# Building one-hot tables in half the steps, with GpSimd taking half of the scaling, in a mixture-of-experts and linear-attention kernel

## Chip, cores and metric

The kernel runs on one core of one Trainium2 chip. The metric is the device time of one launch in microseconds (us); lower is better. Engines are named as in the profile: PE is TensorE, DVE is VectorE, ACT is ScalarE, POOL is GpSimd, SP is SyncE, which only issues DMAs here.

## The reference

Input x has 16 sequences of 512 tokens of 128 features (8192 tokens). After a layer norm, two branches read the same tokens, and their product is added to x.

```python
xn = _layernorm(x, axis=-1)
s = attn(xn)      # token shift, r/k/v projections, 16 heads of 8, chunked decaying state, output projection
g = silu(ffn(xn)) # gates = softmax(xn @ gate_W.T), top 2 of 8 experts
# expert:  (silu(t @ w1_e) * (t @ w3_e)) @ w2_e, width 512, weighed by the gates, 2 per token
# shared:  the same form with w1_s, w3_s, w2_s, applied to all tokens, divided by 8
# ffn = 0.5 * shared + 0.5 * routed
return x + s * g
```

## The kernel before

**Stages.** Normalisation and transposes come first, with the routing logits. Then a feed-forward stage of 62 units, and then 16 attention units. Each matrix product in the feed-forward stage is made of three half-precision products, from a high half and a low half of each operand.

**Units and steps.** A shared unit takes 512 tokens in their own order and is four steps, one for each 128 hidden columns. There are 16. A routed unit takes tokens sorted by expert: 25 wide units (512 rows, four steps) and 21 narrow ones (256 rows, two steps). That makes 206 steps. The list `order` starts with `FIRST = 16 - MIXED` shared units; with `MIXED = 4` these are 12 units, or `FIRST_STEPS = 48` steps (0 to 47). The other four shared units stand among the routed ones. Sorted rows are counted in blocks of 256, 71 in all.

**One step i.** PE makes the two up projections (`pe_up`, 6 matmuls of 512 columns). ACT takes the silu (L781). DVE multiplies it by the second projection (L1218; one input in SBUF, one in PSUM). ACT rounds the product to its high half (L785). The low half is a subtraction of two SBUF tensors, on DVE (`dve_split`, L1222) or on POOL (`pool_first_low`, L624), as `low_on_pool(i)` says: before the change POOL has steps 0 to 11 and then each even step up to 38. PE makes the down projection three steps later (`pe_down`, `LAG = 3`). `pe_up(i)` waits for L1218 of step i-2, and L1218 of step i waits for the low half of step i-2, since `gu` has two buffers.

**Sorting.** To find which token stands in which sorted row, the kernel builds one-hot tables in 16 sets m: `dve_block_set(m)` (L1141, 128x1136, both inputs in SBUF) and `dve_lane_set(m)` (L1151, 128x1024, the same). The block table is scaled by token numbers in two halves of 128x568 (`act_tokens`, L823, two instructions a set). PE multiplies lanes by blocks, 128 products (`pe_hot`, L1498). A set's block table is built in the step that `slot_of` gives, from `HOT_FIRST = 13` over `HOT_SLOTS = 24` steps, its lane table and scaling one step later, and its products at `HOT_LAG = 3`. Behind the last product `dve_source` (L1161 to L1174) makes the gather indices in step 39 and `dve_dest` (L1178 to L1185) the scatter indices in step 40.

**Gather and scatter.** POOL issues two indirect DMAs of 128 rows for each block: gathers into the ring `srows` of `NXB = 3` blocks (`pool_sorted`, L634) and, seven blocks later in its queue, scatters of results (`pool_scatter`, L644). PE transposes a gathered block (`pe_sorted`, L1509, "flip") in the steps of the unit before. The first flip is in step 46 before the change.

**Other work in the steps.** Expert weights come in through a stage of two experts. ACT makes the high halves (`act_split_w`, L766), DVE the low halves (`dve_split_w`, L1013, both inputs in SBUF). `SPLIT_AT` gives the steps: 16 parts over steps 1 to 36 and 8 parts in steps 40 to 47. SP loads expert k only when all parts of expert k-2 are split. The first routed unit waits for all weights. `act_route` (L770, L771, with table loads) stands in step 26 and `dve_gates` (L1201 to L1207) in step 29. From step 75 each fourth step carries a part of the attention projections (`pe_part`, L1596), 32 in all.

Of the kernel before, what the change touches and what calls it, by code (L numbers as in the profile page):

```python
# [69 lines left out]
def build(nc, nb, x, decay, per_head, maa, wT, bias, bias_rows, gateT, w1e, w3e, w2e, w1s, w3s, w2s, const, out):  # L70
# [18 lines left out]
    with ctx:  # L89
# [64 lines left out]

        NXB = 3
        srows = sb("srows", [P, NXB, TPU, P])
# [27 lines left out]
        NBLK = ROUTED * TPU  # L184
        SETS, LANES, LANE_SETS, BLOCK_SETS = 16, 2 * NT // 16, 4, 3
        FOUR = LANES // 2
# [31 lines left out]
        wtmp = early([P, HEADS, Q])  # L218
        same = late([P, HEADS, Q])
        w32r = early([P, P])  # L220
# [70 lines left out]

        MIXED = 4
        FIRST = SHARED - MIXED
# [69 lines left out]
        NHOTS = 2 * NT  # L363
        HOT_FIRST, HOT_SLOTS, HOT_LAG = 13, 24, 3

# [22 lines left out]
        def low_on_pool(i):  # L388
            return i < LOWS_FIRST or (i < HOT_FIRST + HOT_SLOTS + HOT_LAG and i % 2 == 0)

        def lows(i, on_pool):
            return sum(low_on_pool(j) == on_pool for j in range(i + 1))

        LOWS_FIRST = 12
        FIRST_SPLIT = 14
# [9 lines left out]

        LAST_SPLITS = 8
        EARLY_SPLITS = 3 * EXPERTS - LAST_SPLITS
        SPLIT_AT = [1 + j * 38 // EARLY_SPLITS for j in range(EARLY_SPLITS)]
        SPLIT_AT += [FIRST_STEPS - LAST_SPLITS + j for j in range(LAST_SPLITS)]

# [193 lines left out]
        def pool_program(e):  # L604
# [17 lines left out]
            def pool_first_low(i):  # L622
                G.wait_ge(sem["gu_hi"], i + 1)
                G.tensor_tensor(gul[:, i % 4, :], gu[:, i % 2, :], guh[:, i % 4, :], ALU.subtract).then_inc(sem["gu_lo_first"], 1)  # L624

            def pool_sorted(q):
                if q == 0:
                    G.wait_ge(sem["normed_out"], 16 * nb)
                    G.wait_ge(sem["source"], 1)
                if q >= NXB:  # L630
                    G.wait_ge(sem["s_flipped"], q - NXB + 1)
                for t in range(TPU):
                    at = block_at[q] * TPU + t
                    G.indirect_dma_start(srows[:, q % NXB, t, :], None, rows_in,  # L634
                                         bass.IndirectOffsetOnAxis(source[:, at:at + 1], 0)
                                         ).then_inc(sem[f"s_in{q % NXB}"], 16)

# [65 lines left out]
            for b in range(nb):  # L703
                pool_norm(b)
            for i in range(FIRST_STEPS):
                if low_on_pool(i):
                    pool_first_low(i)
# [25 lines left out]
        def act_program(e):  # L733
# [85 lines left out]
            def act_tokens(m):  # L819
                A.wait_ge(sem["hot_block"], m + 1)  # L820
                for k in range(2):
                    half = hot_block[:, m % BLOCK_SETS, k * FOUR:(k + 1) * FOUR, :]
                    A.mul(half, half, C("token")[:, 16 * k + m:16 * k + m + 1]).then_inc(sem["hot_token"], 1)  # L823

# [624 lines left out]
        def pe_program(e):  # L1449
# [44 lines left out]
            def pe_hot(n):  # L1494
                m, k, g = hot_of(n)
                T.wait_ge(sem["hot_set"], m + 1)
                T.wait_ge(sem["hot_token"], 2 * m + k + 1)
                T.matmul(psum[6 + g // 2][:, g % 2 * NBLK:(g % 2 + 1) * NBLK], hot_lane[:, m % LANE_SETS, n % LANES, :],  # L1498
# [230 lines left out]
            for i in range(NS + LAG):  # L1729
                if i < NS:  # L1730
                    pe_up(i)
                    if i == ROUTE_AT:
                        pe_route()
                    for n in hots(i - HOT_FIRST - HOT_LAG):
                        pe_hot(n)
                    for q in flips_at(i):
                        pe_sorted(q)
                if i >= LAG:
                    load = steps[i][0] + 1 if i < NS and last_step_of(i) and routed(steps[i][0] + 1) else None
                    pe_down(i - LAG, load)  # L1740
                if i < NS and part_at(i) is not None:
                    pe_part(part_at(i))
# [47 lines left out]
```

## Time and profile before

| what | value |
|---|---|
| median of 3 runs | 722.61 us |
| runs | 722.04, 722.61 and 2308.06 us |
| span of the profiled execution | 719.3 us |
| PE, DVE, ACT, POOL busy | 91%, 77%, 69%, 67% of the span |
| mean granted TensorE clock | 0.988 |

The span runs from the first to the last instruction of the profiled execution. No separate launch time is listed for that execution; the median lies 3.3 us above its span, and that is taken as what lies around it. The run of 2308.06 us stands alone.

### The profile page before, as it was taken

What the parts mean: (1) busy time and instruction counts of PE and PEld (TensorE: products, weight loads), DVE (VectorE), ACT (ScalarE), POOL (GpSimd) and SP (SyncE); (2) the same over time, 40 slices, a digit from 0 to 9 for tenths busy, and PEclk for the clock granted to TensorE, in tenths of its full rate; (3) what the DMA queues carried; (4) which work ended last, traced back from release to release, by engine and by line L of the source; (5) the groups of instructions that cost most, each with busy time, mean ns of one, the idle gap of its engine ahead of it and who ended that gap; (6) DMA issues with size and microseconds to landing.
All of it is one profiled execution on the core that took longest, in us unless ns stands there. A gap on an engine that the chain in (4) does not pass through costs nothing.

```text
span 719.3 us, 22370 instructions
## 1 busy us (share of the span) xinstructions
PE 654.1 (91%) x8536; PEld 452.1 (63%) x8536; DVE 555.4 (77%) x1058; ACT 494.9 (69%) x1008; POOL 478.9 (67%) x519
## 2 busy tenths in 40 slices
PE   2787897978999999999999999999997899999993
PEld 1544565646665665566666666878886676777772
DVE  5989986877667886667766676667664899999996
ACT  4864798857665656666666666666665788888872
POOL 4844321244777777777777777767778487888873
PEclk9999999999999999999999999999999999999997
DMA  9931111111111323433323334333362767777762
GB/s 243 299 95 45 45 61 46 45 51 36 48 49 49 108 91 108 137 108 108 110 92 109 106 106 139 110 101 108 97 103 93 237 179 230 216 229 222 233 176 59
DMA packets 88616, 86.75 MB, mean 121 GB/s; under 512 B 11394, under 2 KB 65284, under 8 KB 88516
## 3 DMA queue, kind: packets, MB, share of 16 engines
q1 hardware_dynamic: 79428, 66.70, 29.8%
q0 software_dynamic: 9088, 18.63, 9.6%
q8 instruction: 73, 1.20, 0.7%
q14 instruction: 27, 0.22, 0.1%
HBM read 50.82 MB, written 34.47 MB: 119 GB/s over the span
## 4 chain that ended last, share of the span: by engine, by line
PE 53%; DVE 13%; ACT 12%; POOL 11%; issue 7%; DMA 3%; SPq 0%; POOLq 0%; DVEq 0%; ACTq 0%
PE banks L1556 7%; PE banks L1558 7%; PE banks L1557 7%; PE banks L1596 5%; DVE hidden L1218 4%; POOL expert_rows L644 4%; PE banks L1576 4%; PE banks L1577 4%; PE banks L1575 4%; POOL srows L634 3%; ACT hidden L785 3%; PE banks L1621 3%; PE banks L1693 3%; PE banks L1672 3%; ACT rows L823 2%
## 5 line engine op out<-in xcount | busy, mean ns | idle before, releaser
L785 ACT CAST hidden<-hidden 128x512 f16<-128x512 f32 x206 | 127.1, 617 | 135.5 <-DVE hidden L1218 135.4
L634 POOL DMA_INDIRECT srows<-normed_rows,source x142 | 149.7, 1054 | 60.4 <-issue 40.2
L1222 DVE TENSOR_TENSOR hidden<-hidden 128x512 f16<-128x512 f32 x180 | 124.4, 691 | 83.9 <-ACT hidden L785 83.0
L1218 DVE TENSOR_TENSOR hidden<-hidden,banks 128x512 f32<-128x512 f32 x206 | 140.8, 684 | 44.0 <-ACT hidden L781 38.2
L1575 PE MATMUL banks<-wwords,hidden 128*128 (+1 forms) x824 | 148.8, 219 | 1.5 <-DVE hidden L1222 1.1
L1576 PE MATMUL banks<-wwords,hidden 128*128 (+1 forms) x824 | 148.6, 219 | 0.0
L1577 PE MATMUL banks<-wwords,hidden 128*128 (+1 forms) x824 | 148.6, 219 | 0.0
L781 ACT ACTIVATE hidden<-banks 128x512 f32<-128x512 f32 x206 | 122.7, 596 | 28.1 <-PE banks L1558 27.8
L1556 PE MATMUL banks<-sx,wwords 128*128 128x512 f16 (+1 forms) x368 | 121.5, 330 | 3.2 <-DVE wwords L1013 2.7
L1558 PE MATMUL banks<-sx,wwords 128*128 128x512 f16 (+1 forms) x368 | 121.6, 330 | 0.0
L1557 PE MATMUL banks<-sx,wwords 128*128 128x512 f16 (+1 forms) x368 | 121.5, 330 | 0.0
L644 POOL DMA_INDIRECT expert_rows<-ybuf,dest x72 | 77.2, 1072 | 22.8 <-issue 19.8
L1575 PEld LDWEIGHTS banks<-wwords,hidden 128*128 128x128 f16 x824 | 80.6, 98 | 12.4 <-issue 2.0
L644 POOL DMA_INDIRECT expert_rows<-rows,dest x70 | 72.8, 1040 | 23.1 <-issue 20.1
L1576 PEld LDWEIGHTS banks<-wwords,hidden 128*128 128x128 f16 x824 | 80.6, 98 | 11.3
L624 POOL TENSOR_TENSOR hidden<-hidden 128x512 f16<-128x512 f32 x26 | 33.6, 1294 | 76.8 <-ACT hidden L785 76.8
L1303 DVE TENSOR_TENSOR wwords<-banks,wmat 128x1024 f32<-128x1024 f32 x64 | 75.3, 1217 | 10.9 <-PE banks L1672 10.5
L1577 PEld LDWEIGHTS banks<-wwords,hidden 128*128 128x128 f16 x824 | 80.6, 98 | 0.0
L1556 PE MATMUL banks<-xh,wwords 128*128 128x512 f16 x128 | 49.2, 385 | 19.1 <-DVE hidden L1218 18.7
L1321 DVE SCALAR_TENSOR_TENSOR hidden<-banks,cst,hidden 128x256 f32<-128x256 f32 x128 | 61.5, 481 | 3.8 <-ACT hidden L849 0.7
L1558 PEld LDWEIGHTS banks<-sx,wwords 128*128 x368 | 36.0, 98 | 25.6
L1557 PE MATMUL banks<-xl,wwords 128*128 128x512 f16 x128 | 49.0, 383 | 0.0
(218 smaller groups left out, 1429.7 us busy)
## 6 DMA issues: line engine op xcount, KB each, us to landing
rows<-x SPq DMA_DIRECT2D x32, 256.0 KB, 4.9
rows<-expert_rows SPq DMA_DIRECT2D x32, 256.0 KB, 3.6
normed_rows<-rows SPq DMA_DIRECT2D x16, 256.0 KB, 3.9
r_rows<-rows SPq DMA_DIRECT2D x16, 256.0 KB, 2.1
rd_rows<-rows SPq DMA_DIRECT2D x16, 256.0 KB, 2.2
stage<-r_rows SPq DMA_DIRECT2D x16, 256.0 KB, 4.0
k_rows<-rows SPq DMA_DIRECT2D x16, 256.0 KB, 2.2
kd_rows<-rows SPq DMA_DIRECT2D x16, 256.0 KB, 2.2
```

Of the source, the lines that this page charges most:

```text
L634: G.indirect_dma_start(srows[:, q % NXB, t, :], None, rows_in, bass.IndirectOffsetOnAxis(source[:, at:at + 1], 0)).then_inc(sem[f"s_in{q % ...
L644: G.indirect_dma_start(rows_out, bass.IndirectOffsetOnAxis(dest[:, at:at + 1], 0), ring_of(q)[:, t, :], None).then_inc(sem[f"y_stored{q % ...
L781: A.activation(sg[:, i % 2, :], psum[2 * (i % 2)][:, :], ACT.Silu, scale=1.0 / SW).then_inc(sem["silu"], 1)
L785: A.copy(guh[:, i % 4, :], gu[:, i % 2, :]).then_inc(sem["gu_hi"], 1)
L1218: V.tensor_tensor(gu[:, i % 2, :], sg[:, i % 2, :], psum[2 * (i % 2) + 1][:, :], ALU.mult).then_inc(sem["gated"], 1)
L1222: V.tensor_tensor(gul[:, i % 4, :], gu[:, i % 2, :], guh[:, i % 4, :], ALU.subtract).then_inc(sem["gu_lo"], 1)
L1556: T.matmul(o, a, mh, start=True, stop=False)
L1557: T.matmul(o, a, ml, start=False, stop=False)
L1558: k = T.matmul(o, b, mh, start=False, stop=True)
L1575: T.matmul(o, guh[:, i % 4, s], a, start=(j == 0 and n == 0), stop=False)
L1576: T.matmul(o, guh[:, i % 4, s], b, start=False, stop=False)
L1577: k = T.matmul(o, gul[:, i % 4, s], a, start=False, stop=last)
```

## The change

The tables are built over 12 steps in place of 24, one step nearer to their products. POOL scales the second half of each block table, and ACT only the first. POOL makes all low halves of steps 0 to 26, and DVE makes all from step 27 on. `MIXED` becomes 8, so 8 shared units (32 steps) precede the first routed one, and the other 8 stand among the routed units. The gather ring has six blocks. The weight parts stand in other steps: 14 in steps 1 to 25 and 10 in steps 27 to 31, two a step. The block table has four buffers, and the products stand behind the step's down projection.

```diff
-        NXB = 3
+        NXB = 6
-        SETS, LANES, LANE_SETS, BLOCK_SETS = 16, 2 * NT // 16, 4, 3
+        SETS, LANES, LANE_SETS, BLOCK_SETS = 16, 2 * NT // 16, 4, 4
-        same = late([P, HEADS, Q])
+        same = rows[:, 0:HEADS * Q // P, :].rearrange("p a (c i) -> p (a c) i", i=Q)
-        MIXED = 4
+        MIXED = 8
-        HOT_FIRST, HOT_SLOTS, HOT_LAG = 13, 24, 3
+        HOT_FIRST, HOT_SLOTS, HOT_LAG = 13, 12, 2
         def low_on_pool(i):
-            return i < LOWS_FIRST or (i < HOT_FIRST + HOT_SLOTS + HOT_LAG and i % 2 == 0)
+            return i < HOT_FIRST + HOT_SLOTS + HOT_LAG
-        LOWS_FIRST = 12
-        LAST_SPLITS = 8
+        LAST_SPLITS = 10
-        SPLIT_AT = [1 + j * 38 // EARLY_SPLITS for j in range(EARLY_SPLITS)]
-        SPLIT_AT += [FIRST_STEPS - LAST_SPLITS + j for j in range(LAST_SPLITS)]
+        SPLIT_AT = [1 + j * 26 // EARLY_SPLITS for j in range(EARLY_SPLITS)]
+        SPLIT_AT += [FIRST_STEPS - LAST_SPLITS // 2 + j // 2 for j in range(LAST_SPLITS)]
+            def pool_tokens(m):
+                G.wait_ge(sem["hot_block"], m + 1)
+                half = hot_block[:, m % BLOCK_SETS, FOUR:2 * FOUR, :]
+                G.tensor_scalar(half, half, C("token")[:, 16 + m:17 + m], None, ALU.mult).then_inc(sem["hot_token1"], 1)
             for i in range(FIRST_STEPS):
+                for m in block_sets(i - 1):
+                    pool_tokens(m)
                 if low_on_pool(i):
                     pool_first_low(i)
             def act_tokens(m):
                 A.wait_ge(sem["hot_block"], m + 1)
-                for k in range(2):
-                    half = hot_block[:, m % BLOCK_SETS, k * FOUR:(k + 1) * FOUR, :]
-                    A.mul(half, half, C("token")[:, 16 * k + m:16 * k + m + 1]).then_inc(sem["hot_token"], 1)
+                half = hot_block[:, m % BLOCK_SETS, 0:FOUR, :]
+                A.mul(half, half, C("token")[:, m:m + 1]).then_inc(sem["hot_token0"], 1)
             def pe_hot(n):
-                T.wait_ge(sem["hot_token"], 2 * m + k + 1)
+                T.wait_ge(sem[f"hot_token{k}"], m + 1)
                     if i == ROUTE_AT:
                         pe_route()
-                    for n in hots(i - HOT_FIRST - HOT_LAG):
-                        pe_hot(n)
                     for q in flips_at(i):
                         pe_sorted(q)
                 if i >= LAG:
                     load = steps[i][0] + 1 if i < NS and last_step_of(i) and routed(steps[i][0] + 1) else None
                     pe_down(i - LAG, load)
+                for n in hots(i - HOT_FIRST - HOT_LAG):
+                    pe_hot(n)
```

## Rows read from the trace of the kernel before

**Rows 1.** Busy time in four stretches: start:end, length, then each engine.
```profile
42.80:76.80 34.00, 26.58 (x215) 15.02 (x214) 32.70 (x63) 18.60 (x35) 16.12 (x12) 1.00 0.10 30
76.80:110.90 34.10, 30.65 (x294) 19.99 (x293) 30.36 (x50) 28.25 (x51) 8.68 (x7) 1.00 0.16 55
110.90:172.50 61.60, 50.69 (x463) 32.78 (x462) 48.63 (x89) 47.96 (x85) 18.35 (x15) 0.97 0.16 48
172.50:545.00 372.50, 368.09 (x3416) 256.74 (x3415) 260.66 (x435) 240.15 (x465) 282.33 (x269) 1.00 0.32 98
```

**Rows 2.** Timeline of ACT, silus of steps 27, 48, 161 and 162: start, duration.
```profile
117.22 0.60 ACT L781 ACTIVATE hidden<-banks 128x512 f32<-128x512 f32 x1
...
172.51 0.60 ACT L781 ACTIVATE hidden<-banks 128x512 f32<-128x512 f32 x1 [1.61 <-PE banks L1558]
...
440.21 0.60 ACT L781 ACTIVATE hidden<-banks 128x512 f32<-128x512 f32 x1
...
442.18 0.60 ACT L781 ACTIVATE hidden<-banks 128x512 f32<-128x512 f32 x1
```

**Rows 3.** Timeline of DVE in step 20, away from POOL: start, duration.
```profile
97.62 0.68 DVE L1013 SCALAR_TENSOR_TENSOR wwords<-stage,wwords 128x512 f16<-128x512 f32 x1
98.22 0.68 DVE L1151 TENSOR_TENSOR rows<-sx 128x1024 f16<-128x1024 f16 x1
98.82 0.74 DVE L1141 TENSOR_TENSOR rows<-sx 128x1136 f16<-128x1136 f16 x1
```

**Rows 4.** Timeline of all engines where a POOL subtraction meets DVE's lane table.
```profile
133.86 1.43 POOL L624 TENSOR_TENSOR hidden<-hidden 128x512 f16<-128x512 f32 x1 [3.77 <-ACT hidden L785]
134.31 0.69 DVE L1218 TENSOR_TENSOR hidden<-hidden,banks 128x512 f32<-128x512 f32 x1
...
134.38 0.48 PE L1498 MATMUL banks<-rows 128*128 128x142 f16 x5
134.91 0.93 DVE L1151 TENSOR_TENSOR rows<-sx 128x1024 f16<-128x1024 f16 x1
```

**Rows 5.** Timeline where DVE's L1013 meets a POOL subtraction near its start.
```profile
52.06 1.25 POOL L624 TENSOR_TENSOR hidden<-hidden 128x512 f16<-128x512 f32 x1 [0.31 <-ACT hidden L785]
...
52.22 1.64 DVE L1013 SCALAR_TENSOR_TENSOR wwords<-stage,wwords 128x512 f16<-128x512 f32 x1
```

**Rows 6.** POOL's groups by shape: count, busy us, mean ns, idle before.
```profile
L634 POOL DMA_INDIRECT srows<-normed_rows,source x142 | 149.7, 1054 | 60.4 <-issue 40.2 <-PE banks L1509 14.5 <-DVE source L1174 5.7
...
L619 POOL TENSOR_SCALAR rows<-rows,ffn 128x128 f32<-128x128 f32 x48 | 22.3, 476 | 8.1 <-DVE ffn L1000 7.2
...
L698 POOL TENSOR_TENSOR rows<-rows 128x512 f32<-128x512 f32 x15 | 19.2, 1279 | 2.2 <-DVE rows L1330 2.2
...
L650 POOL MEMSET stage<- 128x1024 f32 x1 | 1.0, 971 | 0.0
```

**Rows 7.** Timeline of DVE in step 39, `dve_source` from first to last.
```profile
150.21 0.72 DVE L1161 TENSOR_SCALAR ybuf<-banks 128x142 f32<-128x142 f32 x3
...
153.71 0.68 DVE L1218 TENSOR_TENSOR hidden<-hidden,banks 128x512 f32<-128x512 f32 x1
```

**Rows 8.** DMA issues by tile: median us to landing.
```profile
stage<-w2e SPq DMA_DIRECT2D x8, 256.0 KB, 3.8
```

**Rows 9.** The chain that ended last: an attention part and a flip.
```profile
368.73 1.32 PE banks L1596 x6
...
371.34 0.22 PE banks L1509 x2
```

**Rows 10.** Waits at line L1509: PE idle in total, times.
```profile
  DMA srows<-normed_rows,source: 8.8, 7
```

**Rows 11.** Timeline of ACT: the last unit's result.
```profile
548.88 0.37 ACT L807 COPY rows<-banks 128x256 f32<-128x256 f32 x1 [1.54 <-PE banks L1577]
```

**Rows 12.** Timeline of POOL and SP: the last scatter, the second key load.
```profile
554.04 0.97 POOL L644 DMA_INDIRECT expert_rows<-rows,dest  x1 [0.31 <-issue]
...
557.98 0.43 SPq L519 DMA_DIRECT2D wwords<-kd_rows  x1
```

## The prediction

> **What bounds the kernel now.** I first cut the span at the silus of certain steps and asked for busy time in each stretch [rows 1]. The reader is to see that PE is the bound only from step 48 on: from 172.5 to 545 us it is busy 368.1 of 372.5 us. In steps 0 to 12 (42.8 to 76.8) DVE is busy 32.7 of 34.0, and in steps 13 to 25 it is busy 30.4 of 34.1, with ACT at 28.3. So the first 48 steps hang on DVE and ACT. They take 129.7 us, while PE alone would need 48 x 1.97 = 94.6; 1.97 is a step with neither flip nor attention part, the distance of steps 161 and 162 [rows 2]. Then I read single instructions where POOL and DVE overlap, since the change puts more on POOL beside DVE.
>
> **What a POOL operation does to DVE.** Left alone, DVE starts its operations 0.60 us apart, 0.08 less than they last: L1013 at 97.62, L1151 at 98.22, L1141 at 98.82 [rows 3]; L1141, 0.06 longer, then costs 0.66. In one place POOL's subtraction runs from 133.86 to 135.29. L1218, with one input in PSUM, runs beside it in its usual 0.69. L1151, both of whose inputs are in SBUF, takes 0.93 and ends at 135.84, 0.55 behind POOL's end [rows 4]. Where L1013 meets the subtraction near its start it takes 1.64 in place of 0.68 [rows 3, 5]. So one low half on POOL costs DVE up to 1.64 - 0.68 = 0.96 us, unless DVE is in L1218 or idle. The subtraction itself lasts between 1.25 and 1.43 here [rows 4, 5]; undisturbed I put it at 1.16 (estimate: DVE's second one ends 0.55 behind it, so POOL too will have waited for a table operation at its start).
>
> The Trainium skill, "SBUF — State Buffer", section "Who interferes with whom", says that a VectorE instruction with two SBUF inputs contends with a GpSimd instruction that reads SBUF, and that the later one blocks fully. By that rule, the trace agrees: 0.93 against 0.69, with the end tied to POOL's. The rule speaks against this change, since every table, weight part and low half is such an instruction.
>
> **Steps 0 to 12.** POOL has these low halves already. There are seven weight parts in place of six: one more L1013 on DVE, +0.6 us.
>
> **Steps 13 to 25, the tables.** DVE's own work, by the distances in [rows 3]: 13 L1218 x 0.60 = 7.8; 32 table operations x 0.63 = 20.2; 7 weight parts x 0.60 = 4.2; sum 32.2. POOL gets 13 low halves, up to 0.96 each for DVE, 12.5 us, and 16 scalings of 128x568. The trace has no such scaling on POOL. The nearest row is L619, the same operation on 128x128, 0.48. For the slope, the fill of 1024 elements gives at most 0.971 / 1024 = 0.95 ns an element, and the way from L619 to the 512 elements with two inputs gives (1279 - 476) / 384 = 2.09 ns [rows 6]. The 440 further elements then make 0.89 or 1.40. I take 0.82, just under the lower end, since the scaling reads one tensor and L619's mean holds some waiting. Less 0.20, by which a low half's 1.16 exceeds its price of 0.96, each blocks DVE for 0.62, in sum 9.9 us.
>
> The Trainium skill, "GPSIMD Engine Reference", section "Performance versus the Vector engine", gives about one cycle an element for bodies of one or two operations and about 2.5 as the floor with two inputs. By the page the short duration would be right; no row here shows the scaling itself.
>
> Of the 22.4 us of blocking, the 13 L1218 hide 7.8: a scaling is ready since the end of DVE's step before and can run beside L1218. DVE then needs 32.2 + 14.6 = 46.8 us against 34.1 now: **+12.7**. Bounds are nothing blocked (+1.9, rival A) and the long scaling with nothing hidden (+29.8, rival B). 46.8 is 3.6 a step. PE has 1.97 + 10.7 products x 0.06 (five in 0.48, the last alone 0.23 as a pipelined one, [rows 4]) = 2.6; ACT keeps its 28.3 / 13 = 2.2, with 16 half scalings for some 17; POOL 1.2 + 1.2 x 0.82 and waits. The new waits add nothing by themselves. The scaling waits for a table that DVE finished a step earlier, with low halves queued behind it. PE's products, waiting behind the down projection, hold only the next step's up projection. The fourth block buffer keeps L1141 from waiting for used tables.
>
> **Steps 26 to 47.** Now 61.6 us [rows 1]. Step 26, from 110.9 to the silu of step 27 at 117.22, takes 6.3 because ACT changes tables for the routing exponentials [rows 1, 2]; dve_source holds DVE 3.5 us in step 39 [rows 7]. After the change both stand in step 26 on different engines: 6.3 once. Steps 27 to 31 are DVE's: 5 x (L1218 0.6 + low half 0.6 + two parts 1.2) = 12.0, and for the nine short operations of dve_dest and dve_gates 3.0 (estimate from dve_source, eleven in 3.5): 15.0. The first routed unit waits for the last weights: now 1.6 of idle ACT [rows 2], then 2.2, with two parts in the last step. Steps 32 to 47 go at PE's pace: 16 x 1.97 + 7 flips x 0.22 [rows 9] = 33.1. The loads of the last two experts can begin only behind parts of steps 27 and 28 and are wanted two steps later. A load is three issues, of which the last lands 3.8 behind its issue [rows 8], in sum under 5. Two steps here are 6, but the loads overlap, so the price is 0 to 3; I take 1. Gathers begin at the end of step 26, need 2.7 a block on POOL (two of 1.05 and 0.3 of issue, [rows 6]), and the first flip is four steps off: no wait. Sum 57.6: **-4.0**.
>
> **Steps 48 to 205.** Now 372.5. PE's floor is 157 x 1.97 = 309.3, 32 parts x 1.32 = 42.2 and 69 flips x 0.22 = 15.2 [rows 9], 366.7. The other 5.8 lies in a few steps in which a gathered block comes late: PE waited 8.8 for them [rows 10]. POOL needs 5.4 us a block for four DMAs [rows 6]. With eight shared units among 71 blocks PE takes 47.7 / 8 = 6.0 a block (20 steps, 5 parts, 8 flips), so POOL gets ahead. With 63 flips left and 1 us of stalls this makes 366.4: **-6.1**. What could take it back is POOL's queue order, where a scatter that waits for its result holds the next gather; by the step numbers that leaves a lead of at least two blocks.
>
> **The turn to attention.** The last result is ready at 549.25 [rows 11], but POOL's scatters end at 555.0, and the second key load stands behind them in SP's queue, issued at 557.98 [rows 12]. With POOL ahead, only the last two blocks are left: the one before is ready about a step (1.97) earlier, and two times 2.6 from there end 3.3 behind the last result in place of 5.8: **-2.4**. Next late is that load itself.
>
> **Sum.** 0.6 + 12.7 - 4.0 - 6.1 - 2.4 = +0.8. The span of 719.3 becomes 720.1; with the 3.3 between span and median, 723.4. A measurement of this kernel can tell about 2% (708.2 and 737.1) from no change.
>
> **Rivals.** (A) POOL's new work blocks nothing that matters. For it: L1218 is untouched in [rows 4], and POOL's L619 is short. Against it: [rows 4, 5]. Steps 13 to 25 then take PE's 13 x 2.6 = 33.8 and some waits, 36, or +1.9: 723.4 - 10.8 = 712.6. (B) Slower: on DVE in steps 13 to 25 nothing of the blocking is hidden and the scaling is long. Blocking is 12.5 + 16 x 1.20 = 31.7, the stretch 63.9, +29.8: 740.5. It passes 2% from a net blocking of 28.3 on, in place of 14.6. For it: L1218 of step i+2 waits for the low half of step i, which stands behind scalings on POOL, each of which also waits for a DVE operation. Against it: the blocking has each L1218 to run beside. (C) Weights or first gathers come late on top of the forecast, 3 to 8 us: 729. (D) The tables cost half of what I say and all stalls go: just under 708.
>
> **How the numbers follow.** Forecast 0.50 (716 to 732), A 0.25, B 0.13, C 0.07, D 0.05. The range takes in A and most of B: 710 to 738. Faster by over 2%: D and A's lower edge, 0.08. Slower: B, 0.13. Same: 0.79.
>
> **What the new profile should show.** In steps 13 to 25, 3.6 us a step, with L1141, L1151 and L1013 well above 0.74, 0.69 and 0.68 in the mean; if they stay there, A. POOL's scaling at 0.8, or up to 1.4. One long step, 26, and none at 39. PE's waits for gathered rows near nothing. POOL's last scatter about 3.3 behind the last result. The forecast is wrong if the scaling in half precision costs POOL much more than its single-precision neighbour, or if the blocked time falls into waits that DVE has anyway.

## The result and the profile after

The changed kernel takes **737.5 us** (median of four runs, 734.69 to 738.98) where the kernel before, run beside it, has a median of 722.33. The ratio is 1.0209, with a 95% interval of 1.0182 to 1.0237: slower by 2.1%. It is longer beyond the noise; whether by more than 2% the interval leaves open. The forecast was 723.4, with a range of 710 to 738. So the time lies just inside the upper end, 14 us from the likeliest case and three from rival B (740.5).

The page after begins as follows. The span grew from 719.3 to 736.7, and every engine but POOL has much the same work as before; POOL's share rose from 67% to 70% of a longer span.

```profile
span 736.7 us, 22370 instructions
...
PE 658.8 (89%) x8536; PEld 455.4 (62%) x8536; DVE 562.2 (76%) x1057; ACT 486.5 (66%) x992; POOL 514.0 (70%) x536
```

The view that decides is the one of [rows 1]: the span cut at the silus of steps 0, 13, 26, 48 and 205. Columns as there.

```profile
44.60:80.40 35.80, 27.18 (x214) 15.24 (x213) 33.48 (x63) 19.17 (x35) 15.69 (x12) 0.98 0.13 36
80.40:133.90 53.50, 36.86 (x342) 24.34 (x341) 45.36 (x61) 30.57 (x53) 50.91 (x29) 1.00 0.13 41
133.90:195.10 61.20, 50.12 (x451) 34.52 (x449) 42.36 (x81) 39.07 (x73) 36.40 (x34) 0.92 0.20 59
195.10:560.40 365.30, 365.30 (x3382) 253.27 (x3381) 257.75 (x429) 237.61 (x458) 259.79 (x248) 1.00 0.30 96
```

Side by side, in us (the lengths are differences of the silus' start times to a hundredth, so they differ in the last digit from the rounded windows):

| stretch | before | after | difference | forecast |
|---|---|---|---|---|
| start to step 0 | 42.82 | 44.57 | +1.8 | 0 |
| steps 0 to 12 | 33.98 | 35.85 | +1.9 | +0.6 |
| steps 13 to 25 | 34.12 | 53.48 | **+19.4** | +12.7 |
| steps 26 to 47 | 61.59 | 61.22 | -0.4 | -4.0 |
| steps 48 to 204 | 372.49 | 365.32 | -7.2 | -6.1 |
| step 205 to the end | 174.26 | 176.25 | +2.0 | -2.4 |

Two things stand out. In steps 13 to 25 the busiest engine is POOL, 50.9 of 53.5 us, and not DVE, 45.4. From step 48 on PE is busy for the whole stretch, 365.3 of 365.3. So the routed part does what was forecast and gives 7.2 us, and the table steps cost 19.4.

The groups of DVE and POOL in the table steps, 80.4 to 133.9 (busy us, mean ns of one, then the idle time before them and who ended it). The line numbers of the changed kernel differ a little: L1146 is the block table, L1156 the lane table, L1018 the weight part, L1223 the multiply, L628 POOL's scaling, L623 the low half.

```profile
L1146 DVE TENSOR_TENSOR rows<-sx 128x1136 f16<-128x1136 f16 x16 | 15.8, 1004 | 0.0
L1156 DVE TENSOR_TENSOR rows<-sx 128x1024 f16<-128x1024 f16 x16 | 13.3, 852 | 0.0
L1223 DVE TENSOR_TENSOR hidden<-hidden,banks 128x512 f32<-128x512 f32 x13 | 8.8, 680 | 6.7 <-POOL hidden L623 5.5 <-ACT hidden L787 1.1
L1018 DVE SCALAR_TENSOR_TENSOR wwords<-stage,wwords 128x512 f16<-128x512 f32 x8 | 7.2, 901 | 0.0
L628 POOL TENSOR_SCALAR rows<-rows,cst 128x568 f16<-128x568 f16 x16 | 35.7, 2234 | 0.0
L623 POOL TENSOR_TENSOR hidden<-hidden 128x512 f16<-128x512 f32 x13 | 17.1, 1313 | 3.2 <-ACT hidden L791 3.2
```

Read POOL's two rows first: 16 x 2.23 + 13 x 1.31 = 52.8 us. The last scaling lies mostly behind the window's end, so 50.9 of that fall into its 53.5. The idle time before scalings is 0.0: from the low half at 84.15 on, POOL is never without work that is ready, to the end of the stretch. DVE's own rows show the blocking that the prediction looked for (1004, 852 and 901 ns against 0.74, 0.68 and 0.68 us in [rows 3]), but DVE also stands idle, and what ends most of that (5.5 of 8.1 us) is POOL's low half. DVE waits for POOL's queue, not the other way round.

### The profile page after: what moved, and what is told of

Same layout as the page of the kernel before. It is cut to its first block, busy times and chain, and to the rows that moved or that the text cites. A ratio compares the mean times of both kernels' runs of the same rounds, so it can differ in the third digit from the quotient of the medians.

```text
span 736.7 us, 22370 instructions
## 1 busy us (share of the span) xinstructions
PE 658.8 (89%) x8536; PEld 455.4 (62%) x8536; DVE 562.2 (76%) x1057; ACT 486.5 (66%) x992; POOL 514.0 (70%) x536
## 4 chain that ended last, share of the span: by engine, by line
PE 69%; POOL 10%; DVE 10%; ACT 4%; issue 4%; DMA 2%; SPq 0%; POOLq 0%; DVEq 0%; ACTq 0%
PE banks L1561 10%; PE banks L1563 10%; PE banks L1562 10%; PE banks L1601 6%; PE banks L1580 5%; PE banks L1581 5%; PE banks L1582 5%; POOL rows L628 5%; PE banks L1677 3%; PE banks L1626 3%; PE banks L1698 3%; PE banks L1514 2%; DVE hidden L1223 2%; POOL hidden L623 2%; POOL hidden L674 2%
## 5 line engine op out<-in xcount | busy, mean ns | idle before, releaser
L1223 DVE TENSOR_TENSOR hidden<-hidden,banks 128x512 f32<-128x512 f32 x206 | 140.7, 683 | 43.6 <-ACT hidden L787 34.1
L648 POOL DMA_INDIRECT expert_rows<-ybuf,dest x72 | 75.6, 1050 | 53.0 <-issue 18.3
L1561 PE MATMUL banks<-xh,wwords 128*128 128x512 f16 x128 | 49.5, 387 | 10.8 <-DVE hidden L1223 10.7
L623 POOL TENSOR_TENSOR hidden<-hidden 128x512 f16<-128x512 f32 x27 | 35.0, 1299 | 28.7 <-ACT hidden L791 28.7
L1563 PEld LDWEIGHTS banks<-sx,wwords 128*128 x368 | 36.3, 99 | 25.8
L1561 PEld LDWEIGHTS banks<-sx,wwords 128*128 x368 | 36.2, 98 | 25.1 <-issue 8.3
```

The source lines that it names most:

```text
L648: G.indirect_dma_start(rows_out, bass.IndirectOffsetOnAxis(dest[:, at:at + 1], 0), ring_of(q)[:, t, :], None).then_inc(sem[f"y_stored{q % ...
L1223: V.tensor_tensor(gu[:, i % 2, :], sg[:, i % 2, :], psum[2 * (i % 2) + 1][:, :], ALU.mult).then_inc(sem["gated"], 1)
L1561: T.matmul(o, a, mh, start=True, stop=False)
L1563: k = T.matmul(o, b, mh, start=False, stop=True)
```

## Experiments

The theory after the result, **P**: POOL is the bound in steps 13 to 25, since one scaling costs it far more than forecast. The rival **C**: the pace is set by what POOL's operations cost DVE, as the prediction had it. A third, **L**: it is the time a table takes until PE can use it, whoever scales. Each asks for kernels that take one thing away.

### All scaling on ACT

```diff
-                for m in block_sets(i - 1):
-                    pool_tokens(m)
...
 def act_tokens(m):
-    half = hot_block[:, m % BLOCK_SETS, 0:FOUR, :]
-    A.mul(half, half, C("token")[:, m:m + 1]).then_inc(sem["hot_token0"], 1)
+    for k in range(2):
+        half = hot_block[:, m % BLOCK_SETS, k * FOUR:(k + 1) * FOUR, :]
+        A.mul(half, half, C("token")[:, 16 * k + m:16 * k + m + 1]).then_inc(sem[f"hot_token{k}"], 1)
```

> The changed kernel with both halves of the block table scaled by ACT again; everything else as changed. Theory P (POOL is the bound in the table steps, because one scaling occupies it 2.23 us in the mean): POOL keeps only 13 low halves of 1.3 us, the stretch from step 13 to 26 falls from 53.5 us to what DVE needs, 37 to 39, and the time from 737.5 to about 722. Theory C (DVE held up by POOL is what costs, as I predicted): only the scalings' share of the blocking goes, some 10 us, to 727. Theory L (the tables' latency to PE, whoever scales): no change beyond 3 us.

It took 724.22 us beside 722.63 for the kernel before: ratio 1.0029 (1.0013 to 1.0045). The span is 720.7 and the table steps take 42.8 in place of 53.5. The window of those steps and POOL's one group in it:

```profile
78.60:121.40 42.80, 36.84 (x353) 25.12 (x352) 41.03 (x61) 39.74 (x70) 17.47 (x13) 1.00 0.15 49
...
L623 POOL TENSOR_TENSOR hidden<-hidden 128x512 f16<-128x512 f32 x13 | 17.5, 1344 | 24.4 <-ACT hidden L789 24.4
```

POOL now waits 24.4 us for ACT, and the bound has gone to DVE (41.0 of 42.8), with ACT close behind (39.7). So POOL's scaling costs 10.7 us of the stretch, and 11 to 13 of the whole kernel's 15. That is P, and L is out. But P had put the stretch at 37 to 39; at 42.8 DVE, with low halves on POOL beside it, is later than that. The rest of the change is worth nothing: 1.6 us slower than before.

### Odd low halves back on DVE

```diff
 def low_on_pool(i):
-    return i < HOT_FIRST + HOT_SLOTS + HOT_LAG
+    return i < 12 or (i < HOT_FIRST + HOT_SLOTS + HOT_LAG and i % 2 == 0)
```

> The changed kernel with the low halves of the odd steps 13 to 25 on DVE again; POOL keeps the scalings. Theory P: POOL loses 7 x 1.30 = 9.1 us of work, so about 728. Theory C: DVE gets 7 x 0.60 = 4.2 of work and loses up to 7 x 0.96 = 6.7 of blocking, so 735. Theory L: no change.

730.33 us, ratio 1.011 (1.0077 to 1.0143); table steps 47.5.

```profile
80.50:128.00 47.50, 37.86 (x342) 25.66 (x341) 45.11 (x68) 30.83 (x54) 43.63 (x23) 0.96 0.15 46
...
L628 POOL TENSOR_SCALAR rows<-rows,cst 128x568 f16<-128x568 f16 x16 | 36.8, 2307 | 3.7 <-DVE rows L1146 3.7
```

The time lies between P's 728 and C's 735, nearer to P. Within the window six low halves less on POOL (seven in place of thirteen) save 6.0 us, 1.0 each. POOL is busy for 43.6 us and waits 3.7 for the block tables, 47.3 of 47.5, and DVE is at 45.1: each now holds up the other.

### Weight parts one a step

```diff
-SPLIT_AT = [1 + j * 26 // EARLY_SPLITS for j in range(EARLY_SPLITS)]
-SPLIT_AT += [FIRST_STEPS - LAST_SPLITS // 2 + j // 2 for j in range(LAST_SPLITS)]
+SPLIT_AT = [1, 2, 4, 6, 8, 10, 12] + [6 + j for j in range(7, 3 * EXPERTS)]
```

> The changed kernel with one weight part a step from step 13 to 29, in place of every second step and then two a step in 27 to 31; the loads of the last two experts begin behind steps 20 and 23. Theory P: DVE and ACT have room beside POOL in the table steps, so that stretch stays at 53.5, and the long steps 30 and 31 (6.6 and 5.4 us) fall to 2.5 to 3.5: -6 to -8 us, 730. Theory C: DVE is full in the table steps and six more parts cost 3.6 there: 734. If loads weren't what was late, no change.

729.94 us, ratio 1.0104 (1.0075 to 1.0133), so 7.6 less than the changed kernel. The two windows are steps 13 to 25 and 26 to 47:

```profile
80.30:135.50 55.20, 39.97 (x341) 26.03 (x340) 50.16 (x68) 33.87 (x60) 51.18 (x29) 0.96 0.22 66
135.50:188.50 53.00, 48.11 (x451) 33.63 (x449) 39.29 (x75) 35.73 (x67) 34.99 (x34) 0.98 0.15 39
```

DVE does five microseconds more in the table steps (50.2 against 45.4), and the stretch grows by 1.6 only: while POOL is the bound, DVE's work there is nearly free. Steps 26 to 47 give back 8.2 us (53.0 against 61.2). Two things are in these 8.2: six weight parts less to be split there, at the prediction's 0.6 each 3.6 us, and last loads that are issued earlier, the other 4.6. This is an estimate; the two were not run apart. For late loads the prediction had allowed 1 us.

### The gather ring alone

The kernel before with one line changed, `NXB = 3` to `NXB = 6`.

> The kernel before with the gather ring of six blocks alone. If the ring is what removes the late gathered blocks (8.8 us of PE waiting before, 1 to 2 after), 2 to 5 us faster, near 719. If it is the earlier start of POOL and the eight shared units in between, no change: 722.

722.65 us, ratio 1.0005 (0.9986 to 1.0024). Steps 48 to 204 take 372.52 as before. The larger ring by itself gives nothing. What frees the 7.2 us in the changed kernel is then its other side, eight shared units among the routed ones and gathers that have begun earlier, or the two together. A kernel with those and a ring of three was not run.

### Four kernels in a second comparison

In this comparison and the two after it **the kernel before itself took 827.7, 830.4 and 819.1 us**, in place of 722.6. The kernel before was not profiled there, but two kernels with nearly its code were. In them the steps 0 to 47 take 129.7 and 129.8 us, as long as in [rows 1], and the attention part 175.1 and 176.8; steps 48 to 204 take 482.5 and 480.8 in place of 372.5. So whole times of these comparisons are read only against their own kernel before, and the table steps are read from the windows. The last section comes back to it.

**The scaling alone** is the kernel before, tables over 24 steps, with the second half of each block table scaled by POOL.

```diff
+                for m in block_sets(i - 1):
+                    pool_tokens(m)
...
 def act_tokens(m):
-    for k in range(2):
-        half = hot_block[:, m % BLOCK_SETS, k * FOUR:(k + 1) * FOUR, :]
-        A.mul(half, half, C("token")[:, 16 * k + m:16 * k + m + 1]).then_inc(sem["hot_token"], 1)
+    half = hot_block[:, m % BLOCK_SETS, 0:FOUR, :]
+    A.mul(half, half, C("token")[:, m:m + 1]).then_inc(sem["hot_token0"], 1)
```

> The kernel before (24 steps of tables) with the second half of each block table scaled by POOL in place of ACT, and nothing else. Theory P: POOL has 16 x 2.0 + 13 x 1.3 = 49 us of work in the 72 us of steps 13 to 39 and isn't full, and ACT loses 16 x 0.66 = 10.6: between no change and 4 us faster, 719 to 723. Theory C: DVE is held up by 16 x 0.6 = 10 us more: 730.

827.88 us beside 827.7, ratio 0.9992 (0.9961 to 1.0023): no change. Steps 13 to 25, in which half of the sets stand, and POOL's group over all 24 steps:

```profile
76.85:111.18 34.33, 29.95 (x292) 19.87 (x291) 32.21 (x50) 23.81 (x44) 25.25 (x15) 1.00 0.18 55
...
L629 POOL TENSOR_SCALAR rows<-rows,cst 128x568 f16<-128x568 f16 x16 | 32.8, 2053 | 8.8 <-DVE rows L1147 8.8
```

The scaling costs 2.05 us here too, but POOL has room (25.3 of 34.3), and the stretch is 0.2 longer than before. DVE's busy time rises by 1.8 and ACT's falls by 4.4, neither of which shows in the time. C, which had 7.5 us more, fails here. So a scaling beside DVE does not cost much by itself; it costs in steps in which POOL has nothing left.

**Half of POOL's scaling** is the changed kernel with the last quarter of each block table on POOL (128x284). ACT scales the first half and, in a second instruction, the third quarter; the cut shows POOL's line only.

```diff
-    half = hot_block[:, m % BLOCK_SETS, FOUR:2 * FOUR, :]
+    half = hot_block[:, m % BLOCK_SETS, FOUR + 2:2 * FOUR, :]
```

> The changed kernel with POOL scaling one quarter of each block table (128x284) and ACT three quarters. Theory P: by 0.44 at 128 and 1.70 at 568 elements a quarter is 0.9 alone, some 1.2 beside DVE; POOL's work falls from 52.6 to 13 x 1.3 + 16 x 1.2 = 36, so DVE is the bound and the time is near the one with all scaling on ACT, 724 to 727. If the cost is the number of meetings with DVE and not the length, 732 or more.

The table steps take 45.8, between 42.8 (none on POOL) and 53.5 (all).

```profile
78.50:124.30 45.80, 36.73 (x343) 24.45 (x341) 45.70 (x61) 36.67 (x70) 41.37 (x28) 1.00 0.14 43
...
L628 POOL TENSOR_SCALAR rows<-rows,cst 128x284 f16<-128x284 f16 x15 | 24.0, 1606 | 0.7 <-DVE rows L1148 0.7
```

DVE is busy for all of it (45.7 of 45.8) and POOL for 41.4. POOL's own work is down by 9.5, but the stretch only by 7.7, since DVE is late next. P had put POOL's work at 36 and the stretch near 42.8; both came out longer, since a scaling of half the length still takes 1.61. By the two lengths measured below a quarter table alone would take 0.60 + 156 x 2.5 ns = 0.99 (estimate), so it loses 0.6 beside DVE, and the scaling of twice the length loses 2.23 - 1.70 = 0.5. DVE is busy for 45.7 with quarters, 45.4 with halves and 41.0 with none. So by these two lengths what the engines lose to each other goes by how often they meet, and hardly by the scaling's length. The whole time, 860.0 (ratio 1.0397, 1.0324 to 1.0471), carries the loss behind step 32 that is told below.

**Scaling on ACT and weights one a step together** is the first and the third edit in one.

> Both: all scaling on ACT and one weight part a step from step 13 to 29. If the two costs lie in separate stretches they add up: 737.5 - 13.3 - 7.6 = 716.6. But with POOL unloaded DVE is full in the table steps, and six more parts of 0.6 there give back 3.6: 718 to 720.

871.93 us, ratio 1.0535 (1.0474 to 1.0596). The plain sum failed where it can be read without the loss: the table steps take 48.0, not the 42.8 of the first experiment, nor 42.8 + 3.6 as expected for six parts of 0.6. With POOL free, DVE is the bound, and six more weight parts cost 48.0 - 42.8 = 5.2 us; in the third experiment the same parts had cost 1.6. Two gains measured one at a time, each with another engine as the bound, do not add.

**The scaling by itself**: the kernel before with 14 scalings on a scratch tile at the head of POOL's queue, each waiting for the one before. DVE has no table and no weight part beside them; from 3.7 us on it works on the normalisation, and the scalings before and after that point take the same 1.70.

```diff
+def pool_cost():
...
+    G.memset(scratch[:, :], 1.0).then_inc(sem["cost"], 1)
...
+    for o, a, s in ((a16, a16, one), (a32, a32, one), (a16, a32, one), (a32, a16, one), (a16, a16, 1.0), (w16, w16, one), (w32s, w32s, one)):
+        for k in range(2):
+            G.wait_ge(sem["cost"], n)
+            G.tensor_scalar(o, a, s, None, ALU.mult).then_inc(sem["cost"], 1)
...
```

> The kernel before with 14 scalings on POOL ahead of everything, while DVE has no work, on a scratch tile: two each of 568 elements half precision in place, single in place, half out of single, single out of half, half in place with a constant factor; and 128 elements half and single. If half precision is what makes the scaling slow, single 568 takes 0.9 to 1.4 and half 1.7. If it is the price of any scaling with a factor from a tile, all of 568 take 1.7 and the one with a constant less. The output's time is not of interest; the work on the scratch tile is extra.

All fourteen stand in one row of their line (the three numbers behind the colon are the shortest, median and longest in ns):

```profile
L618 POOL TENSOR_SCALAR scratch<-scratch x14: 602/1701/1709, 1.7 to 21.5; 128x568 f16<-128x568 f16 x4, 128x568 f32<-128x568 f32 x2, 128x568 f16<-128x568 f32 x2, 128x568 f32<-128x568 f16 x2
```

At 568 elements it takes 1.70 us, and the same for every mix of half and single precision; with a constant in place of the factor from a tile it takes 1.63. At 128 elements it is 0.60. The slope is (1.70 - 0.60) / 440 = 2.5 ns an element. The Trainium skill, "GPSIMD Engine Reference", section "Performance versus the Vector engine", puts bodies of one or two operations at 1.03 cycles an element. At the 1.2 GHz that it reckons with this is an estimate of 0.86 ns; the measured 2.5 is nearly three times that, and decides.

### A version between the two kernels

Since neither side of the change paid, I tried a mixture: 18 table steps and six shared units ahead (40 steps), all scaling on ACT, even low halves on POOL, the weights split over 31 steps, the ring of six.

```diff
-MIXED = 8
+MIXED = 6
...
-HOT_FIRST, HOT_SLOTS, HOT_LAG = 13, 12, 2
+HOT_FIRST, HOT_SLOTS, HOT_LAG = 13, 18, 2
...
```

> A version in between: 6 shared units stand among the routed ones (40 steps ahead of the first routed one), the tables over 18 steps, all scaling on ACT, low halves on POOL in steps 0 to 11 and each even step to 32, weight parts 16 in steps 1 to 30 and one a step in 32 to 39, ring of six. Theory P with what the runs showed: the first 48 steps hang on DVE's total work, so they take the 172.5 us of before within 3, and the routed steps keep the gain of 7: 714 to 719. If the gain of the routed steps needs eight shared units among them, 722.

> The kernel with one quarter of each block table scaled by POOL, once more, since the kernel before took 827 us in that comparison, with waits in the routed steps that no other run has. In that profile the scaling took 1.59 in the mean and the table steps 45.8 us, against 53.5 with a half and 42.8 with none on POOL. So I expect 727 beside a kernel before of 722.

> All scaling on ACT and one weight part a step from step 13 to 29, once more for the same reason. In that profile the table steps took 48.0 us against 42.8 without the earlier parts, so 5.2 of the 7.6 us of gain are given back: 721 to 722, where 716.6 would be the two edits added up.

> The version with 18 table steps and six shared units among the routed ones, once more, since its first comparison also fell where the kernel before takes 830 us. There its steps 0 to 26 took 72.7 us against 68.1 of the kernel before and 78.4 with twelve table steps and all scaling on ACT. If the kernel before takes 722 here: 714 to 719 if the routed steps gain their 7 us and the first 48 steps end within 3 us of 172.5; 722 or more if they end at 178 as with twelve steps. If it takes 830 again, 3% to 4% slower as before.

The last three repeat kernels from above; in neither comparison did the kernel before take 722 us. The mixture took 865.0 beside 830.37 (1.0371, 1.0301 to 1.0442) and 858.91 beside 819.12 (1.041, 1.0337 to 1.0483), half of the scaling 858.77 (1.0328, 1.0253 to 1.0403), act and weights 866.65 (1.0479, 1.0395 to 1.0563). The table steps repeat to 0.02 us: 37.0 and 37.0 for the mixture, 45.8 and 45.8 for half of the scaling, 48.0 and 48.0 for act and weights. The window of the mixture and of act and weights, steps 13 to 25:

```profile
78.60:115.60 37.00, 32.89 (x309) 21.67 (x308) 34.76 (x57) 32.54 (x59) 9.43 (x7) 1.00 0.18 56
```

```profile
78.60:126.60 48.00, 40.00 (x350) 26.24 (x349) 47.39 (x67) 42.89 (x75) 19.56 (x13) 0.96 0.25 77
```

No version that was run beats the kernel before. Whether the mixture would, where the kernel before takes 722, is open.

## Why the prediction was right or wrong

The whole time came inside the range, but the likeliest case, 723.4, missed by 14 us, and the sum was wrong in a place that matters. That the range held is in part luck: its upper end was set by rival B's price for blocked DVE time, which did not come, while POOL as the bound and the late loads, which did, filled the same room.

**Steps 13 to 25: the step that failed.** It is the one that reads "I take 0.82" for a scaling, and with it the line that gives POOL "1.2 + 1.2 x 0.82 and waits" a step, some 2.2. The scaling takes 1.70 alone and 2.23 beside DVE, outside even the upper end of 1.40 that the rows had given. With 2.23, POOL needs 1.31 + 16 / 13 x 2.23 = 4.1 a step, 53 us for thirteen, and is the bound.

Two things are in this step. The first is the price alone: 1.70 in place of 0.82. It would not have been enough, for 13 low halves of 1.16 and 16 scalings of 1.70 are 42.3 us, less than the 46.8 that the prediction gave DVE. The second is that POOL loses time to DVE too (2.23 in place of 1.70, 1.31 in place of 1.16), 10.5 us in sum; the prediction reckoned with the loss on DVE's side alone. For the price, the slopes were the error. The fill and the two-input operation gave 0.95 and 2.09 ns an element; the true slope is 2.5, steeper than both. A memset and a subtraction are other operations, and the distance from one of them to another shape of a third is no slope of it. Nor is L619 "the same operation": it multiplies and adds, with a factor and a term from a tile, where the scaling only multiplies.

DVE's term, by contrast, was near: forecast 46.8 of work and blocking, measured busy 45.4. It came out right for a wrong reason, by two errors that cancel. Its 32.2 of DVE's own work left out the short operations of these steps, four casts and the routing's rest, some 3.5 us:

```profile
L1137 DVE CAST sx<-sx 128x128 f16<-128x128 int32 x4 | 1.8, 514 | 0.0
```

With them its price for the low halves comes out: 32.2 + 3.5 + 12.5 less 7.8 hidden is 40.4, and with no scaling on POOL DVE is busy for 41.0. The scalings add 45.4 - 41.0 = 4.4, 0.3 each, where the prediction had 9.9. The prediction let every scaling block DVE for all but 0.20 of its length. By that rule 1.70 would block for 16 x 1.50 = 24.0, which with the low halves' 12.5 less 7.8 hidden makes DVE's stretch 60.9. The trace shows that a scaling holds DVE for far less. In the timeline of the changed kernel, a scaling that starts just ahead of L1223, and one that starts beside a weight part:

```profile
104.82 1.70 POOL L628 TENSOR_SCALAR rows<-rows,cst 128x568 f16<-128x568 f16 x1
104.94 0.69 DVE L1223 TENSOR_TENSOR hidden<-hidden,banks 128x512 f32<-128x512 f32 x1 [1.12 <-POOL hidden L623]
105.55 0.69 DVE L1018 SCALAR_TENSOR_TENSOR wwords<-stage,wwords 128x512 f16<-128x512 f32 x1
106.15 0.68 DVE L1156 TENSOR_TENSOR rows<-sx 128x1024 f16<-128x1024 f16 x1
...
114.09 2.62 POOL L628 TENSOR_SCALAR rows<-rows,cst 128x568 f16<-128x568 f16 x1
...
115.14 1.20 DVE L1146 TENSOR_TENSOR rows<-sx 128x1136 f16<-128x1136 f16 x1
```

The first scaling lasts its 1.70, and a weight part and a lane table, both with two SBUF inputs, run beside it in their usual 0.69 and 0.68. The second one takes 2.62, and the block table beside it 1.20 in place of 0.74. The pairs at 90 to 98 us are alike: POOL's scalings take 2.65 and 2.72, and DVE's block table at 92.58 takes 1.20.

```profile
90.35 1.16 POOL L623 TENSOR_TENSOR hidden<-hidden 128x512 f16<-128x512 f32 x1
91.49 2.65 POOL L628 TENSOR_SCALAR rows<-rows,cst 128x568 f16<-128x568 f16 x1
94.11 1.16 POOL L623 TENSOR_TENSOR hidden<-hidden 128x512 f16<-128x512 f32 x1
95.25 2.72 POOL L628 TENSOR_SCALAR rows<-rows,cst 128x568 f16<-128x568 f16 x1
```

So a scaling loses up to 1.0 us in these rows to DVE's operations and costs DVE about 0.5, where a low half costs DVE up to 0.96 of its 1.16, as [rows 5] had it. The rule of the Trainium skill on two SBUF inputs that the prediction cited, "SBUF — State Buffer", section "Who interferes with whom", names the later instruction as the one fully blocked; for the low half the traces agree (1.64 in [rows 5]), for the scaling they show the milder and mutual loss above. The low half undisturbed was put at 1.16, and it is 1.16 in these rows.

**Rival B** ended near the measured time with the wrong mechanism. It had DVE as the bound and the blocking not hidden, 63.9 us; DVE was busy for 45.4. Its argument, that L1218 waits for a low half "which stands behind scalings on POOL", is what happened: most of DVE's idle time ends on POOL's low half. **Rival A** (nothing blocked, 36 us) is ruled out: with no scaling on POOL at all the table steps still take 42.8. The prediction also read [rows 1] too narrowly: in steps 13 to 25 and 26 to 47 of the kernel before PE is as busy as DVE (30.7 against 30.4, and 50.7 against 48.6), so that these steps "hang on DVE and ACT" does not follow from busy time alone.

**Steps 0 to 12**, +0.6 forecast, +1.9 measured. All kernels with six weight parts there take 33.98 or 33.99, and those with seven 35.66 to 35.85. One more weight part costs 1.7, not 0.60. In the changed kernel none of these parts takes more than 1.08 us. But three operations of the routing that stand behind parts now meet a low half on POOL and take 1.64 or 1.65 (L1039, L1043 and L1047), where before two operations did, one of them the part of [rows 5]. So 0.60 and one meeting at 0.96 come near the 1.7, but it is the order of the two queues that decides which operation meets what. This is read from the trace and was not tested. The prediction had [rows 5] and priced the part as if nothing shifted behind it.

**Steps 26 to 47**, -4.0 forecast, -0.4 measured. The third experiment shows the term: with the weights split earlier the stretch takes 53.0. By the prediction's own terms, 57.6 less 1 for late loads and less 3.6 for six parts, it should take 53.0. So the other terms hold in sum, and "0 to 3; I take 1" for the last loads should have been 4.6. In the changed kernel the last expert's loads are issued late and land late, and everything behind them waits. The queue of SP, then ACT:

```profile
145.47 0.33 SPq L471 DMA_DIRECT2D stage<-w1e  x1
145.84 1.35 SPq L471 DMA_DIRECT2D stage<-w3e  x1
147.23 0.43 SPq L471 DMA_DIRECT2D stage<-w2e  x1
```

```profile
152.34 0.63 ACT L772 ACTIVATE wwords<-stage 128x512 f16<-128x512 f32 x1 [3.65 <-DMA stage<-w2e]
```

ACT stands 3.65 us for that load. PE's longest wait in the steps follows from it, 7.5 us at the first routed up projection, for the last low part of the weights (the view's rows on these waits):

```profile
PE banks L1561 <- DVE wwords L1018: 7.5, 1, 7.5
DVE hidden L1223 <- POOL hidden L623: 5.5, 3, 2.8
ACT wwords L772 <- DMA stage<-w2e: 4.0, 2, 3.6
```

PE's wait has an echo. Its granted clock, 1.00 of full speed before, stood at half, the lower level of 1.2 GHz, from 151.8 to 162.0 us, after PE had stood idle from 149.0 on (this is the 0.92 in the row of 133.9 to 195.1). Step 32, in that time, took 3.6 us, against 2.0 at the full clock in the third experiment.

The prediction's rival C was the one for this (weights late on top of the forecast, 3 to 8 us), held at 7%. It happened together with the long table steps and not in place of them. The last term of the stretch held: from step 33 to step 47 it takes 32.2 in the changed kernel, in all of the first three experiments too (32.2 to 32.3), at PE's pace as forecast.

**Steps 48 to 204**, -6.1 forecast, -7.2 measured. Right, by its own mechanism: PE's waits for gathered rows fell from 8.8 [rows 10] to 0.9.

```profile
  DMA srows<-normed_rows,source: 0.9, 2
```

The fourth experiment adds that the ring of six alone gives none of it. The prediction had put it on POOL getting ahead, and not on the ring.

**The turn to attention**, -2.4 forecast, +2.0 measured. The mechanism held. The last result is ready at 564.37 + 0.37 = 564.74, and POOL's last scatter ends at 566.94 + 0.97 = 567.91, 3.2 behind it (forecast 3.3; 5.8 before). The second key load is issued at 571.13, 10.7 behind the silu of step 205 at 560.44, where it was 13.0 before [rows 12].

```profile
564.37 0.37 ACT L813 COPY rows<-banks 128x256 f32<-128x256 f32 x1 [1.59 <-PE banks L1582]
```

```profile
566.94 0.97 POOL L648 DMA_INDIRECT expert_rows<-rows,dest  x1 [0.31 <-issue]
```

```profile
571.13 0.43 SPq L518 DMA_DIRECT2D wwords<-kd_rows  x1
```

But the gain of 2.3 there does not last: over the next attention units it is lost again, and the end comes 2.0 later. Kernels whose code is the same from there on vary as well: 174.3 to 175.5 us for before and six of the variants, 176.0 to 177.2 for after and four others, and the mixture took 179.5 in one execution and 176.3 in the other. So the +2.0 cannot be told from what differs between executions, and what is known of the wait that was forecast is that it fell by 2.3 and that the 16 units behind it did not end earlier by that. What sets that time is open.

**The start**, +1.8 and not forecast: PE's granted clock stood at half between 39.2 and 46.0 us, just ahead of step 0. The kernels of the second and third experiment show the same start (44.8 and 44.7, with the clock at half up to 45.2 and 45.3), those of the first and most later ones, with the same code there and the full clock, 42.8 to 43.0. It differs between executions, and its cause is open.

The sum by the measured terms, for the likeliest case: scaling at POOL's 2.23 in place of 0.82 gives +19.4 in place of +12.7 (6.7), weights +3.6, start +1.8, steps 0 to 12 +1.3, end +4.4, routed steps -1.1, together 16.7, and the span's 720.1 + 16.7 is 736.8 against 736.7. That it closes shows nothing by itself, since each term is a measured stretch less its forecast; what stands apart from it is POOL's 52.8 us of measured work in a stretch of 53.5.

## What to carry to other kernels

Before work is moved to an engine, sum that engine's own queue over the stretch with a duration of that very operation and shape, measured beside the work that it will stand beside. A price pieced together from other operations missed by a factor of two, the time lost beside DVE added a third to it, and the two together changed the bound. Each edit's worth depends on which engine is the bound at that time: the same six weight parts cost 1.6 us while POOL was the bound and 5.2 when DVE was, so edits measured one by one are not to be added. And where a stretch is packed tighter, look up when the last load for its end is issued: 1 us was allowed for late loads where 4.6 were lost.

## What the runs showed of the hardware

**Scaling on POOL takes the same time in half and in single precision.** It is 1.70 us for 128x568 in half precision, in single precision, and between the two. A half-precision table gives POOL nothing back. At 128x128 it took 0.60 when each waited for the one before; the 0.48 of [rows 6], where they follow one another, is another operation (a multiplication and an addition), so what the waiting costs was not measured.

**Not all POOL work blocks DVE alike.** The two-input subtraction held up DVE's two-input operations by up to 0.96 us; the one-input scaling held one up by 0.5 and let two others pass at full speed, and lost 0.9 to 1.0 itself where it collided.

**One kernel, two very different times.** In the second to fourth comparison the kernel before took 827.7, 830.4 and 819.1 us in place of 722.6. From the kernel with the scaling alone, whose first 48 steps are as long as before's in the first comparison to within 0.3 us in each stretch, steps 26 to 47 and then 48 to 204:

```profile
111.18:172.55 61.37, 53.02 (x466) 34.47 (x464) 49.50 (x89) 43.50 (x77) 34.45 (x23) 0.93 0.17 48
172.55:655.08 482.53, 411.14 (x3420) 265.66 (x3419) 262.00 (x435) 239.25 (x466) 273.34 (x271) 0.95 0.25 76
```

The same instructions take 482.5 in place of 372.5 [rows 1], with PE busy for 411.1 at a mean granted clock of 0.95 and idle for the other 71. Its idle time is in many short pieces. Between 180 and 540 us there are 56.2 us of it, 47.0 of them in 57 pieces of over 0.4 us, where the kernel before in the first comparison has 4 such pieces and 4.1 us. Of the 57, 44 (34.3 us) end on nothing the profile shows, as in the second row below, and the others on a DVE operation. ACT in turn waits for something outside the trace (times and longest behind the sum):

```profile
ACT hidden L788 <- remote: 85.9, 35, 4.9
```

```profile
308.86 0.38 PE L1564 MATMUL banks<-sx,wwords 128*128 128x512 f16 x1 [1.03 <-issue]
```

It begins with the first routed unit, in every kernel of these comparisons. So those that start the routed units after 32 or 40 steps in place of 48 lose more: with 32, steps 33 to 47 take 43.8 to 44.7 us in place of 32.2. That is why the ratios of those comparisons, 1.033 to 1.053, say little of the edits themselves. The cause is open. The first and the fourth comparison, 722.6 and 819.1, are listed under the same chip number, the other two under two others, so the chip's number does not part them. The instruction queues moved the same 73 and 27 packets in both, and a gather's issue on POOL took 1.01 us against 1.05 in the mean, so neither of these has grown.
